# Linear attention on one core: a quad's scores in two pairs of heads, each waiting for one mask

## What is computed

```python
q, k, v = (proj(wq), proj(wk), proj(wv))
q = (q @ fq1_w.T + fq1_b) * (q @ fq2_w.T + fq2_b)
k = (k @ fk1_w.T + fk1_b) * (k @ fk2_w.T + fk2_b)
...
inter = jnp.einsum('bhncd,bhnde->bhnce', qc, kv)
s = jnp.einsum('bhncd,bhnmd->bhncm', qc, kc)
s = jnp.where(mask, s, 0.0)
intra = jnp.einsum('bhncm,bhnmd->bhncd', s, vc)
o = (inter + intra).reshape(B, H, L, dk)
o = o * jax.lax.rsqrt(jnp.mean(o * o, axis=-1, keepdims=True) + EPS) * norm_w
return o @ wo.T
```

## Time and profile before

| | |
|---|---|
| median of three runs | 1040.65 us |
| the profiled execution | 1037.62 us |
| its span, first instruction to last | 1035.8 us |
| mean granted TensorE clock | 0.965 of full |
| TensorE, VectorE, ScalarE, GpSimd busy | 940.4, 695.1, 461.2, 373.9 us |
| masks of this stage | 32, from 42.5 us on, the last starting at 90.8 us |

### The profile page before, as it was taken

One profiled execution on the slowest core, in us unless ns is written; L12 is line 12 of the kernel. 1 busy time (PEld: TensorE's weight loads), 2 busy tenths in 40 slices (PEclk: granted clock), 3 DMA queues, 4 the chain that ended last, 5 costly groups with the idle time before them and its releaser, 6 DMA issues. The chain is left out here.

```text
span 1035.8 us, 18280 instructions
## 1 busy us (share of the span) xinstructions
PE 940.4 (91%) x7007; PEld 778.2 (75%) x7017; DVE 695.1 (67%) x1172; ACT 461.2 (45%) x1041; POOL 373.9 (36%) x364
## 2 busy tenths in 40 slices
PE   8788989988999999999999889999999778999970
PEld 5555656656888888888887568889889647999960
DVE  3466767876574655566554799768877575888846
ACT  4322435545545445644545344443323333666630
POOL 2000400003756666666673165554444123000005
PEclk9889969999999999999999999999999989999995
DMA  4000100004433433233331111040000128655513
GB/s 181 0 2 2 31 1 2 2 1 166 120 107 94 112 108 107 83 113 108 108 108 36 46 42 47 17 163 1 2 1 1 35 92 287 239 201 198 202 36 117
DMA packets 56885, 85.84 MB, mean 83 GB/s; under 512 B 4960, under 2 KB 47712, under 8 KB 54624
## 3 DMA queue, kind: packets, MB, share of 16 engines
q1 hardware_dynamic: 55264, 80.48, 24.2%
q0 software_dynamic: 1536, 4.20, 1.3%
HBM read 73.65 MB, written 11.01 MB: 82 GB/s over the span
## 5 line engine op out<-in xcount | busy, mean ns | idle before, releaser
L1640 ACT ACTIVATE e_probs<-ps,e_neg_max 128x256 f32<-128x256 f32 (+1 forms) x128 | 52.1, 419 | 125.3 <-DVE e_neg_max L1570 125.3
L1151 DVE TENSOR_TENSOR d_s_m<-ps,d_decay 128x768 f32<-128x768 f32 x64 | 58.3, 952 | 46.8 <-PE ps L1333 46.8
L123 PE MATMUL ps<-xTl,d_wh 128*128 128x512 f32 x192 | 79.5, 414 | 0.6 <-DVE xTl L577 0.5
L123 PE MATMUL ps<-xTh,d_wh 128*128 128x512 f32 x192 | 76.1, 396 | 0.0
L123 PE MATMUL ps<-xTh,d_wl 128*128 128x512 f32 x192 | 75.8, 395 | 0.0
L1246 ACT ACTIVATE d_gated_hi<-d_gated 128x512 fp32r<-128x512 f32 x32 | 20.2, 633 | 115.6 <-DVE d_gated L1157 115.6
L123 PE MATMUL ps<-wl_gated,f_wh 128*128 128x256 f32 x240 | 69.7, 290 | 2.1 <-issue 2.1
L1527 POOL TENSOR_TENSOR e_q_T<-xT 128x512 f32<-128x512 f32 x32 | 41.1, 1284 | 82.1 <-DVE xT L1558 82.1
L123 PE MATMUL ps<-wh_gated,f_wl 128*128 128x256 f32 x240 | 67.9, 283 | 0.0
L123 PE MATMUL ps<-wh_gated,f_wh 128*128 128x256 f32 x240 | 67.9, 283 | 0.0
L815 ACT ACTIVATE g_probs<-ps,g_neg_max 128x256 f32<-128x256 f32 (+1 forms) x128 | 43.2, 422 | 40.1 <-DVE g_neg_max L751 40.1
(11 more groups left out here) (368 smaller groups left out, 3069.3 us busy)
## 6 DMA issues: line engine op xcount, KB each, us to landing
f_stage<-in_w_experts SPq DMA_DIRECT2D x15, 1536.0 KB
d_decay<-in_decay SPq DMA_DIRECT2D x32, 384.0 KB, 3.7
d_stage<-in_w_decay SPq DMA_DIRECT2D x32, 256.0 KB, 3.2
d_stage<-in_w_decay SPq DMA_DIRECT2D x32, 128.5 KB, 3.5
d_stage_v<-in_w_decay SPq DMA_DIRECT2D x32, 128.0 KB, 2.3
d_stage<-in_w_decay SPq DMA_DIRECT2D x32, 128.0 KB, 2.5
slot_rows<-warm SPq DMA_DIRECT2D x1, 3840.0 KB, 13.2
slot_outs<-f_rows SPq DMA_DIRECT2D x15, 256.0 KB, 2.1
```

What stands on the lines that cost most here:

```text
L123: mm = pe.matmul(out, w(k), x(k), start=(n == 0), stop=(n == 3 * len(ks) - 1))
L1151: dve.tensor_tensor(s_m[:, s % 2, 2 * b:2 * b + 2, :], ps[:, 2 + 2 * b:4 + 2 * b, 0:CAUSAL], decay[:], ALU.mult).then_inc(sm_ready, 1)
L1640: ex = act.activation(probs[:, s % KEPT, i, cols], ps[:, 2 + i, cols], ACT.Exp, bias=neg_max[:, s % 4, t, i:i + 1], accum_out=sums[:, s % ...
```

## The change

`scores` issues heads 0 and 1 with all their products, then heads 2 and 3. Each pair waits for one mask of the quad before, the one that reads its two banks, and each pair signals. `masks` waits for its own pair before each of its two instructions. The products, banks and masks are the same.

```diff
             def masks(b, quad):
                 n = QUADS * b + quad
-                dve.wait_ge(s_ps, n + 1)
                 need(dve, pv_ps, n - KEPT + 1)
                 for two in range(2):
+                    dve.wait_ge(s_ps, 2 * n + two + 1)
                     dve.tensor_tensor(s_m[:, n % KEPT, 2 * two:2 * two + 2, :], ps[:, 2 + 2 * two:4 + 2 * two, 0:CAUSAL],
...
                 if n == 0:
                     pe.wait_ge(f_ready, seconds(len(mapped)))
-                need(pe, sm_ready, 2 * n)
-                groups = [(ps[:, 2 + g, :], slice(ROWS * g, ROWS * (g + 1))) for g in range(4)]
-                for bank, rows in groups:
-                    pe.matmul(bank[:, 0:SEQ], k_map[rows, m, b * SEQ:b * SEQ + P], q_par[rows, par, m, tok], start=True, stop=True)
-                for bank, rows in groups:
-                    mm = pe.matmul(bank[:, SEQ:CAUSAL], k_map[rows, m, late], q_par[rows, par, m, late], start=True, stop=True)
-                mm.then_inc(s_ps, 1)
+                for two in range(2):
+                    need(pe, sm_ready, 2 * (n - 1) + two + 1)
+                    groups = [(ps[:, 2 + g, :], slice(ROWS * g, ROWS * (g + 1))) for g in (2 * two, 2 * two + 1)]
+                    for bank, rows in groups:
+                        pe.matmul(bank[:, 0:SEQ], k_map[rows, m, b * SEQ:b * SEQ + P], q_par[rows, par, m, tok], start=True, stop=True)
+                    for bank, rows in groups:
+                        mm = pe.matmul(bank[:, SEQ:CAUSAL], k_map[rows, m, late], q_par[rows, par, m, late], start=True, stop=True)
+                    mm.then_inc(s_ps, 1)
```

## The result

| | before | change |
|---|---|---|
| median, us | 1040.88 (4 runs) | 1034.63 (4 runs, 1034.51 to 1035.51) |
| ratio, 95% interval | | 0.9948 [0.9926, 0.9971] |
| the same in a later comparison | 1038.80 (35 runs) | 1034.48 (12 runs), 0.9957 [0.9940, 0.9973] |
| profiled execution, its span, us | 1037.62, 1035.8 | 1034.65, 1032.8 |
| batch 0, first mask to first mask | 13.80 | 12.81 |

The account below looks back on a forecast made before the run. In linear attention neither VectorE nor TensorE is full; they hand four score banks to and fro. Batches 0 to 3 sum as -3.0 + 0.0 + 0.3 + 0.3 = -2.4 us, from 1040.65 to 1038.25 us; 8-in-10 range 1034.5 to 1041.8.

Parts of the forecast that it names:

- first rival, clock rival: Linear attention: clock stays at 2.4 GHz, saving 4.8 us in batch 0, 1.6 in batch 1; total 1034.85 us; chance 0.20.
- the rounds of batch 0: Sign: first masks in batch 0 some 2.0 us apart at 2.4 GHz and 2.7 at 1.2 GHz.
- the waits: Sign: VectorE's waits for scores fall from 15.0 to about 11 us, TensorE's for masks from 12.1 to 4 or less.
- quad 4's first mask: Sign at the end of batch 0: it comes near 53 us, where it stood at 56.31 before.
- batch 2: Sign: it takes near 12.0 us, 11.70 before; over 12.5 us would show the forecast wrong.
- The price of a second pair: TensorE: scores of a quad's second two heads, queued directly behind the first two, add 0.60 us at 2.4 GHz.
- Batches 2 and 3: TensorE's list of work grows from 9.6 to 12.0 us and decides; each batch gets 0.3 us longer.
- Batch 0: Earlier hand-over of banks brings quad 4's first mask forward; 3.0 us saved, between cases of 2.5 and 3.5.
- second rival: Clock returns only at 55.2: batch 0 saves 1.2 us, batches 2 and 3 lose 0.6 each; total 1040.65; chance 0.25.
- Batch 1: Has room and handovers to save, but an earlier clock fall finds more TensorE work queued; no change, 0.0 us.
- slower rival: TensorE becomes the bound at a low clock, batch 1 over 14 us; sum +2.8 us, total 1043.45; chance 0.10.

## Why the prediction was right, and where not

The median, 1034.63 us, lies in the range (1034.5 to 1041.8), 0.13 us from its lower edge; that is luck. It misses the forecast's own range of 1036.2 to 1040.4; the wide range reaches so far down only for the first rival, and that one's step did not come true as a whole. The direction, which had a chance of 0.50, holds, and so does its cause, the early hand-over of two banks. The forecast was -2.4 us, measured were -4.3 to -6.2. Of its signs, the rounds of batch 0 (1.99, 2.70 and 2.72 us) and the waits (9.9 and 2.0) came out; quad 4's first mask (55.39 instead of near 53) and batch 2 (11.06 instead of near 12.0) did not. By the forecast's own steps:

- **The price of a second pair** (0.60 us, bounds 0.55 and 0.76) is the term that failed. The lower bound itself was wrong: it priced a second pair as a further stream behind the first. Where it is free to follow, it streams beside it, for 0.01 to 0.03 us (the rows at 84.46, and 0.10 us a batch where both pairs waited for both masks). Kept apart, it costs 0.83. In a batch of the change two second pairs are free and two wait for their masks, 1.0 us in all where the forecast had 2.4.
- **Batches 2 and 3** were to lengthen by 0.3 us each and shortened by 0.64 and 0.67. TensorE's list is still nearly the whole of the batch (10.95 busy of 11.06), but it grew by 1.0 us, to some 10.6 by the forecast's pieces (9.6, an estimate), and not to 12.0. The 9.60 and 10.04 of 11.62 us that the prediction gives for batch 2 are of the window 80.28 to 91.90, which is batch 3's.
- **Batch 0** was to save 3.0 and saved 0.99 (1.62 in the second profile). The round at 1.2 GHz (2.70 to 2.72 us against 2.75) came out, and with it quad 3's first mask (49.99, forecast 50.0); the last round, forecast at 3.8 us, took 5.40. Quad 3's second pair had to wait for its mask, so it ran alone and handed over at 51.30, not 50.8; and the clock came back at 54.9, not near 52, so that both groups of values and a part of quad 4's scores ran at 1.2 GHz. It is the step of the second rival (clock back at 55.2, 1.2 saved) that came true here.
- **Batch 1** was put at 0.0 and saved 2.22. Its hand-overs are worth 0.74 (11.80 to 11.06), and the missing stretch at 1.2 GHz the rest, about 1.5. In the second profile of the change that stretch is there (from 63.4 on) and batch 1 takes 12.69 us (54.56 to 67.25).
- **The clock rival** (2.4 GHz throughout, 1034.85) gave the right total by the wrong step. The clock fell at 44.7, after 3.2 us in which TensorE was busy 2.06, and stayed low for 10.2 us although TensorE's records then have no gap. The Trainium skill's rule that activity releases the throttle (TensorE: Matmul & The Clock Gate, Part 1, "What's actually happening") agrees with the profiles in which idle products stood in batch 0 and the clock stayed up, 9.65 of 9.70 us busy in the first. It does not agree with the 10.20 of 10.20 here, nor with the 13.50 of 13.50 in which idle products stood as well; busy time as the records show it, with its covered waits, does not tell these cases apart. What the rival had for batch 1, no low stretch, came true in the first profile of the change and not in the second.
- **The slower rival** did not come: batch 1 took 11.06 and 12.69 us in the two profiles, below its 14. Its estimate of 15 us, a pure loss of one group's time a quad, took it for given that pairs issued one after the other no longer run at once; the rows at 84.46 show that they do.
- **The sum against the runs.** The two profiled executions differ by 3.0 us, the stage alone by 4.45. The next low clock stretch, 137 to 154 before, became one of 10.2 us,

```profile
133.40:143.60 10.20, 8.61 (x38) 6.20 (x38) 5.04 (x9) 5.30 (x17) 0.00 (x0) 0.50 0.00 0
```

by which the lead grew to 7.2 us at 155; it shrank again in later stages, where the change had stretches at 1.2 GHz of its own (597.7 to 600.9, and 884.4 to 891.1). Where such stretches fall differs between profiles of one kernel too. Over all fourteen profiles, of before, the change and the experiments, the time from the stage's end to the end of the span lies between 930.8 and 936.3 us (932.7 before, 934.1 in the change): the next stage starts 0.32 us behind this one as the prediction has it, but what the total shows of the stage's gain is uncertain by that much in a single execution. That the medians differ by more than these two profiles is consistent with the execution shown of before being faster than every one of its four timed runs; what share of the 4.3 to 6.2 us belongs to later stages was not isolated.

## What to carry to other kernels

When one engine fills banks and another empties them in several instructions, signal and wait for each instruction's own banks, on both sides; one side alone gave nothing here. Row tiles of TensorE that were issued in two groups still ran beside one another here when nothing stood between the groups. So splitting the packed group was free where its later half need not wait, and cost nearly its whole length (0.83 of 0.86 us) where a product over the full array came between. And before pricing the wait, look at the granted clock: in the profile of the change half of what the hand-over was worth in batch 0 was lost at 1.2 GHz, not in the rounds that it shortened but in the one where TensorE's list was the limit.

## What was not expected of the hardware

Products in different rows of the array ran beside one another even across groups that the program issues one after the other, the first records of two pairs 0.03 us apart. The clock stayed at 1.2 GHz for 10.2 us, and once for 13.5 us, in which TensorE's records have no gap, and it fell in different places in different executions of the same program (44.7 and 42.9 us in two profiles of the change), which moved single batches by 1.6 us (batch 1: 11.06 and 12.69).
